# Grouped attention scores as pairs of 48-row matmuls on two row halves of the TensorE array, with the projections regrouped between the pairs

## The chip, the cores and the metric

The kernel runs on one core of one Trainium2 chip. The metric is the device time of one execution in microseconds (us), as the median of several runs. Everything below that is read per engine comes from one profiled execution.

## What is computed

A gated cross-attention block and a gated feed-forward block, on 8 batches of 256 tokens of 512 numbers, all in float32. The reference, cut to what matters:

```python
x = x + tanh(g_xattn[0]) * xattn(layernorm(x), ctx, ctx, Wq, Wk, Wv, Wfc, bfc)
x = x + tanh(g_ffn[0]) * ffn(layernorm(x), router_weight, ...)
# xattn: 32 query heads of 16, in 8 groups that share one key and one value head
score = einsum('bhqd,bhkd->bhqk', qh, kh) / sqrt(16)
out = einsum('bhqk,bhkd->bhqd', softmax(score), vh)
return out.reshape(N, S, 512) @ Wfc.T + bfc
# ffn: SwiGLU of 2048 plus a routed one of 256, weighted by the softmax of the two best logits
```

## The kernel before

**Precision.** A float32 product is made of three matmuls in the format fp32r: each operand is split into a high part (rounded) and a low part (the rest), and `three` (L1234 to L1238) adds high x low, low x high and high x high in PSUM. For the scores the same three products are one matmul: the 16 numbers of a head stand three times on the contraction rows, q as high, high, low and k as high, low, high.

**Attention.** T = 2048 tokens are 4 blocks of 512 (two batches each). A block has 8 steps: 2 batches x 4 chunks of 8 heads. Step n has 8 units. For each unit u TensorE runs:
- `sm_unit(n + 2, u)` (L1291): scores of the step two ahead with queries on the partitions, two matmuls of 256 columns into bank 0 or 1. VectorE takes their row maximum (`maximum`, L880, into `mcol`), and nothing else uses them. A maximum waits for its own unit; `sm_unit` u waits for the maximum of u - 2.
- `st_unit(n, u)` (L1301): scores of this step with keys on the partitions, one matmul of 512 columns into bank 2 or 3. A row of q_st holds minus the maximum, so the subtraction is part of the matmul (66 rows: 48 of data, filler, the row of maxima). ScalarE writes exp of them to `probs` (L733). `st_unit` u waits for the exp of u - 2.
- at u = 1 and u = 5 two `pv_unit` each (L1311): probabilities x values in four column strips of 32, bank 4. After the last of a step VectorE transposes, divides and transposes back (`o_turn` L985, `inverse` L989, `divide` L995 and L1000), ScalarE and VectorE split the result (`a_high`, `a_low`).
- at u = 2 `mt_job` (L1241): the 128 x 16 maxima of step n + 1 are turned, ScalarE copies them (`m_copy`, L652), and two DMAs put them in their row of q_st (`put_max`, L300).

**What lies between the units.** Into the units of the same body the projections of the neighbouring blocks are written by hand, a quarter of a product (`part`, three matmuls of 512 columns) at most after a unit: q of the next block (16 parts), k and v (8 parts), the output projection Wfc of this block (16 parts), and the transposes of the normalised x (`x_job`) and of v (`vt_job`). They share banks 6 and 7 (PJ). Each is followed by a high split on ScalarE and a low one on VectorE.

**DMA.** All DMAs are issued by one queue, SyncE's, in program order. q and k of a block go to DRAM (`q_scr`, `k_scr`) and come back with 16 partitions per part: `read_q` fetches the q of step n + 3 when the scores of step n - 1 are made, `read_k` the keys of a batch.

**Feed-forward.** 36 hidden blocks in pairs, with Strassen sums for gate and up, the weights split on GpSimd while the products run. GpSimd makes the split input of this stage during the last attention block, from `x2_copy` on.

## Time and profile before

| | |
|---|---|
| median of 3 runs | 955.46 us (954.95 to 959.87) |
| the profiled execution | 962.23 us, of which 960.4 us are the span of the trace |
| busy in the span: TensorE / VectorE / GpSimd / ScalarE | 916.6 / 649.1 / 485.7 / 343.8 us |
| attention: start to the first score step | 0 to 54.9 us |
| attention: blocks 0, 1, 2 | 87.6, 86.8 and 86.6 us |
| attention: block 3, to the first feed-forward product | 77.0 us |
| feed-forward | 567.5 us |

The stages are read from the table of stretches, and the boundaries are the starts of the first exp of a block. An engine's busy time is the union of its instructions. A matmul's shown length includes its way through the array, so the distance from one start to the next is what a matmul costs in a stream.

### The profile page before, as it was taken

The page shows a single profiled execution, that of the slowest core. Times are in us where ns is not written, and L with a number is a line of the kernel's source. Part 1 is how long each engine was busy: PE and PEld are TensorE (multiplying, and loading weights), DVE is VectorE, ACT ScalarE, POOL GpSimd, SP SyncE. Part 2 cuts the span into 40 slices and gives each one's busy share as a digit, 9 for nine tenths or more (in the row PEclk, how much of TensorE's full clock was granted, in tenths as well). Part 3 has the DMA queues.
Part 4 walks back from the last instruction along what each step waited for, and adds up shares of the span by engine and source line. Part 5 has one row for each costly group of instructions (what it writes and reads, how often), then busy time and mean ns, then how long its engine had stood idle before and what let it go on. Part 6 is the DMA issues. An engine that isn't in the chain of part 4 may idle for free.

```text
span 960.4 us, 14872 instructions
## 1 busy us (share of the span) xinstructions
PE 916.6 (95%) x4896; PEld 707.4 (74%) x4896; DVE 649.1 (68%) x1084; ACT 343.8 (36%) x637; POOL 485.7 (51%) x483
## 2 busy tenths in 40 slices
PE   4699999998999999989999999999999999999998
PEld 3566666676667665568888888888688888888887
DVE  6567888877877688466656665566866655666566
ACT  5156566555655577321212212134422111221111
POOL 4201301300130179785668866685588666786650
PEclk9758999999999799989999999999999999999999
DMA  7862335325353320211112121121321211212102
GB/s 272 172 165 67 85 100 89 101 68 111 77 98 77 73 44 12 87 48 61 44 44 66 44 66 44 44 67 44 110 67 45 66 44 44 65 45 64 44 1 87
DMA packets 42346, 70.83 MB, mean 74 GB/s; under 512 B 5312, under 2 KB 21184, under 8 KB 42048
## 3 DMA queue, kind: packets, MB, share of 16 engines
q1 hardware_dynamic: 42304, 70.29, 27.6%
q8 instruction: 24, 0.39, 0.2%
q14 instruction: 18, 0.15, 0.1%
HBM read 55.33 MB, written 14.68 MB: 73 GB/s over the span
## 4 chain that ended last, share of the span: by engine, by line
PE 72%; issue 17%; DVE 6%; POOL 2%; ACT 1%; DMA 1%; SPq 0%; POOLq 0%; DVEq 0%; ACTq 0%
PE bank L1236 20%; PE bank L1237 20%; PE bank L1238 20%; PE bank L1291 4%; PE bank L1311 3%; PE bank L1301 3%; PE bank L1241 2%; DVE mcol L880 1%; POOL xa L461 1%; POOL cx_l L430 1%; PE bank L1560 1%; DVE x_l L1199 1%; DMA q_st<-q_scr 1%; DMA xa<-x 1%; DVE xa L1084 0%
## 5 line engine op out<-in xcount | busy, mean ns | idle before, releaser
L880 DVE TENSOR_REDUCE mcol<-bank 128x2 f32<-128x512 f32 x256 | 170.1, 678 | 56.7 <-PE bank L1291 55.9
L1236 PE MATMUL bank<-x_l,w_h 128*128 128x512 f32 x504 | 198.1, 393 | 7.1 <-DVE u L1072 3.7
L733 ACT ACTIVATE probs<-bank 128x512 f32<-128x512 f32 x256 | 150.4, 594 | 130.2 <-PE bank L1301 129.3
L1237 PE MATMUL bank<-x_h,w_l 128*128 128x512 f32 x504 | 196.7, 390 | 0.0
L1238 PE MATMUL bank<-x_h,w_h 128*128 128x512 f32 x504 | 196.7, 390 | 0.0
L588 ACT ACTIVATE hT_h<-bank 128x512 fp32r<-128x512 f32 x72 | 43.1, 599 | 365.4 <-DVE bank L1172 356.6
L545 POOL TENSOR_TENSOR w_l<-raw,w_h 128x512 fp32r<-128x512 f32 (+1 forms) x144 | 161.9, 1157 | 2.9
L1084 DVE SCALAR_TENSOR_TENSOR xa<-bank,tgf,xa 128x512 f32<-128x512 f32 x128 | 96.2, 751 | 79.2 <-PE bank L1238 79.1
L1291 PEld LDWEIGHTS bank<-k_st,q_st 65*128 65x128 f32 x512 | 95.7, 207 | 45.6 <-DVE mcol L880 17.0
L1291 PE MATMUL bank<-k_st,q_st 65*128 65x256 f32 x512 | 117.2, 319 | 12.4 <-DMA q_st<-q_scr 8.0
L1236 PEld LDWEIGHTS bank<-x_l,w_h 128*128 128x128 f32 x504 | 94.8, 188 | 31.5 <-DVE u L1072 4.9
L430 POOL TENSOR_TENSOR cx_l<-cx_raw,cx_h 128x512 fp32r<-128x512 f32 x12 | 15.6, 1296 | 198.0 <-ACT cx_h L588 198.0
L1236 PE MATMUL bank<-dn_l,hT_h 128*128 128x512 f32 x288 | 112.8, 392 | 0.0
L1237 PE MATMUL bank<-dn_h,hT_l 128*128 128x512 f32 x288 | 112.7, 391 | 0.0
L1238 PE MATMUL bank<-dn_h,hT_h 128*128 128x512 f32 x288 | 112.6, 391 | 0.0
L1238 PEld LDWEIGHTS bank<-x_h,w_h 128*128 128x128 f32 x504 | 94.9, 188 | 19.8
L1237 PEld LDWEIGHTS bank<-x_h,w_l 128*128 128x128 f32 x504 | 94.9, 188 | 19.2
L1301 PE MATMUL bank<-q_st,k_st 66*128 66x512 f32 x256 | 105.3, 415 | 1.8 <-ACT probs L733 1.8
L1072 DVE TENSOR_TENSOR u<-bank,r 128x512 f32<-128x512 f32 x72 | 49.8, 691 | 70.9 <-PE bank L1238 70.9
L554 POOL CAST dn_h<-dnraw 128x512 fp32r<-128x512 f32 x36 | 22.0, 612 | 121.3 <-PE bank L1238 99.6
L542 POOL CAST w_h<-raw 128x1792 fp32r<-128x1792 f32 x36 | 63.6, 1767 | 28.3 <-DVE x_l L1199 16.7
L1311 PE MATMUL bank<-probs,vals 128*32 128x256 f32 x1024 | 73.7, 408 | 0.0
(146 smaller groups left out, 1376.1 us busy)
## 6 DMA issues: line engine op xcount, KB each, us to landing
raw<-w_gu SPq DMA_DIRECT2D x36, 512.0 KB, 3.3
q_st<-q_scr SPq DMA_DIRECT2D x96, 128.0 KB, 3.8
dnraw<-w_dn SPq DMA_DIRECT2D x36, 256.0 KB, 2.7
xa<-x SPq DMA_DIRECT2D x4, 1024.0 KB, 7.9
cx_raw<-ctxT SPq DMA_DIRECT2D x16, 256.0 KB, 3.5
q_scr<-qx_h SPq DMA_DIRECT2D x16, 256.0 KB, 2.1
q_scr<-qx_l SPq DMA_DIRECT2D x16, 256.0 KB, 2.2
out<-xa SPq DMA_DIRECT2D x16, 256.0 KB, 2.0
```

The source lines that it names most:

```text
L542: g.tensor_copy(w_h[f][:, :, :], raw[f][:, 0:7, :]).then_inc(gu_hi, 1)
L545: last = g.tensor_tensor(w_l[f][:, part, :], raw[f][:, part, :], w_h[f][:, part, :].bitcast(f32), ALU.subtract)
L733: nc.scalar.activation(probs[:, p, 2 * (u % 2):2 * (u % 2) + 2, :], STB[u % 2][:, :].rearrange("p (r q) -> p r q", r=2), ACT.Exp, scale=fl ...
L880: v.tensor_reduce(mcol[:, par, at:at + 2], bank[u % sm_banks(n)][:, :].rearrange("p (r k) -> p r k", r=2), AX.X, ALU.max).then_inc(max_ok, 1)
L1072: return v.tensor_tensor(out, psum[:, :], part[:, :], ALU.add)
L1084: v.scalar_tensor_tensor(tile, source[:, :], scale, tile, ALU.mult, ALU.add).then_inc(acc_ok, 1)
L1236: mm(out, a_h, b_l, start=start, stop=False, skip_group_check=onto)
L1237: mm(out, a_l, b_h, start=False, stop=False, skip_group_check=onto)
L1238: return mm(out, a_h, b_h, start=False, stop=stop, skip_group_check=onto)
L1291: last = mm(bank[u % banks][:, j * S:(j + 1) * S], q_st[0:SM, c, h, qt * P:(qt + 1) * P], k_st[0:SM, bb, 2 * c + g2, :], start=True, stop= ...
L1301: mm(STB[u % 2][:, :], k_st[0:ST, bb, 2 * c + g2, kt * P:(kt + 1) * P], q_st[0:ST, c, h:h + 2, :], start=True, stop=True).then_inc(st_full, 1)
L1311: last = mm(OTB[32 * r:32 * r + VW, g2 * S:(g2 + 1) * S], vals[:, bb, kt, 2 * c + g2, :], probs[:, p, r, :], start=kt == 0, stop=kt == 1)
```

## The change

- **Row halves.** A chunk's 8 heads are two halves of four (the columns of Wq are put in another order on the host, so that each group's heads are spread over both). Half e stands on partitions 64e to 64e + 47, its row of maxima on 64e + 48. q_st holds 4 heads side by side in place of 8, k_st the keys twice. There is no filler any more: the contraction is 48 rows for sm and 49 for st, where it was 65 and 66.
- **Pairs.** `sm_pair` v is the former units 2v and 2v + 1: four matmuls of 256 columns, alternately on the two row halves and into the two banks 0 and 1. `st_pair` is two matmuls of 512 columns. `sm_pair` v waits for the maxima of both units of pair v - 1, `st_pair` for both exps. Maxima and exps are as many and as large as before.
- **Projections.** The same parts as before, now in runs of up to four after pairs 1 and 3 only, and at other steps: after pairs 1 and 3 the parts of steps 0 to 7 of a middle block are 2+1, 1+2, 2+4, 0+4, 4+3, 3+3, 3+4 and 4+0 (q, k, v and Wfc), besides four transposes of x after each of the four places of steps 0 and 1 and two of v in steps 2 and 7. x, k and q of the later chunks use bank 6 alone, the rest bank 7.
- **ScalarE and VectorE** get the splits at other units; aT has two buffers; some splits are made one to three steps later.
- **DMA.** `read_q` is 6 DMAs of 64 KB (it was 3 of 128 KB) and waits for the probabilities x values of step n - 1; `read_k` is 6 DMAs of 128 KB (it was 3). At step 5 the queue holds 2 writes of q, 6 reads of k, 6 reads of q and 2 of maxima.
- **Start and end.** The zero fill of q_st is gone, the fill of k_st covers 128 partitions; the first weights of the feed-forward (w_h0, w_l0) have memory of their own, so GpSimd does not wait for step N - 2 before it splits them.

```diff
+CONSTS = 1
+SM = 3 * DH
 MROW = SM
 ST = MROW + 1
+ROWS = P // 2
+QUADS = HC // 2
 VW = 32
...
+        w_h0 = sb("w_h0", [P, 7, SLOT], f32r)
+        w_l0 = sb("w_l0", [P, 7, SLOT], f32r)
...
+        q_st = sb("q_st", [P, CHUNKS, QUADS, S], f32r, att)
         k_st = sb("k_st", [P, 2, GROUPS, S], f32r, att)
         vT = sb("vT", [P, BLOCK], f32, att)
...
+        aT = sb("aT", [P, 2, S], f32, att)
         tbias = sb("tbias", [P, D], f32, att)
...
-        sm_full, max_ok = sem("sm_full"), sem("max_ok")
+        sm_full, st_full, max_ok = [sem("sm_full0"), sem("sm_full1")], [sem("st_full0"), sem("st_full1")], sem("max_ok")
...
-            return bank[j] if isinstance(tb, int) and tb == 0 else PJ[j % 2]
-
-        def split_unit(s):
-
-            return 5 if s in (3, 6, 7) else 4
+            return bank[j] if isinstance(tb, int) and tb == 0 else PJ[0]
+
+        def q_bank(tb, oc):
+
+            return PJ[(oc + 1) % 2] if isinstance(tb, int) and tb == 0 else PJ[1 if oc == 0 else 0]
+
+        def f_bank(t, bb, qt):
+
+            return PJ[qt] if isinstance(t, int) and t == BLOCKS - 1 and bb == 1 else PJ[1]
...
+            def scored(n):
+
+                sp.wait_ge(pv_ok, 4 * n)
...
-                    sp.wait_ge(st_full, UNITS * n)
+                    scored(n)
                 sp.wait_ge(q_wr[c], 32 * (tb + 1))
-                for row, part in ((0, 0), (DH, 0), (2 * DH, 1)):
-                    src = q_scr[part, tb, c, :, bb * S:(bb + 1) * S].rearrange("(h d) q -> d h q", d=DH)
-                    sp.dma_start(r(q_st[row:row + DH, c, :, :]), src).then_inc(q_rd[c], 16)
+                for e in range(2):
+                    for row, part in ((0, 0), (DH, 0), (2 * DH, 1)):
+                        src = q_scr[part, tb, c, e * ROWS:(e + 1) * ROWS,
+                                    bb * S:(bb + 1) * S].rearrange("(h d) q -> d h q", d=DH)
+                        at = e * ROWS + row
+                        sp.dma_start(r(q_st[at:at + DH, c, :, :]), src).then_inc(q_rd[c], 16)
 
...
                 sp.wait_ge(k_wr, 32 * (tb + 1))
-                for row, part in ((0, 0), (DH, 1), (2 * DH, 0)):
-                    src = k_scr[part, tb, :, bb * S:(bb + 1) * S].rearrange("(g d) s -> d g s", d=DH)
-                    sp.dma_start(r(k_st[row:row + DH, bb, :, :]), src).then_inc(k_rd[bb], 16)
+                for e in range(2):
+                    for row, part in ((0, 0), (DH, 1), (2 * DH, 0)):
+                        src = k_scr[part, tb, :, bb * S:(bb + 1) * S].rearrange("(g d) s -> d g s", d=DH)
+                        at = e * ROWS + row
+                        sp.dma_start(r(k_st[at:at + DH, bb, :, :]), src).then_inc(k_rd[bb], 16)
...
-                for qt in range(2):
-                    sp.dma_start(r(q_st[MROW:MROW + 1, slot, :, qt * P:(qt + 1) * P]),
-                                 r(mT[qt * HC:(qt + 1) * HC, :])).then_inc(m_rd, 16)
+                for e in range(2):
+                    at = e * ROWS + MROW
+                    sp.dma_start(r(q_st[at:at + 1, slot, :, :].rearrange("p h (t q) -> p (h t) q", q=P)),
+                                 r(mT[e * HC:(e + 1) * HC, :])).then_inc(m_rd, 16)
 
             x_v = x.rearrange("(t j p) d -> t p j d", p=P, j=TILES)
...
                     n = STEPS * t + s
-                    if s + 3 < STEPS or not last and s != 6:
+                    if s == 0 and not first:
+                        write_q_high(t, 3)
+                        write_q_low(t, 3)
+                    if not last and s >= 5:
+                        write_q_high(t + 1, s - 5)
+                        write_q_low(t + 1, s - 5)
+                    if s == 5 and not last:
+                        read_k(t + 1, 0)
+                    if s + 3 < STEPS or not last:
                         e = s + 3
                         tb = t if e < STEPS else t + 1
                         read_q(tb, e % STEPS // CHUNKS, e % CHUNKS, n, first and s == 0)
-                    if not last:
-                        if s == 4:
-                            write_k(t + 1)
-                        if s == 6:
...
-            g.memset(q_st[0:SM, :, :, :].bitcast(f32), 0.0).then_inc(consts, 1)
...
             def split_gu(G, f):
-                if isinstance(G, int) and G < 2:
-                    pool.wait_ge(st_full, UNITS * (N - 2) if G == 0 else UNITS * N)
-                else:
+                if is_at(G, 1):
+                    pool.wait_ge(st_full[0], UNITS // 2 * N)
+                    pool.wait_ge(st_full[1], UNITS // 2 * N)
+                if not (isinstance(G, int) and G < 2):
                     pool.wait_ge(full[3], G - 1)
...
             def maximum(n, u, par):
                 qt, g2, half = u // 2 % 2, u // 4, u % 2
-                dve.wait_ge(sm_full, UNITS * n + u + 1)
+                dve.wait_ge(sm_full[half], UNITS // 2 * n + u // 2 + 1)
                 if u == 0 and not (isinstance(n, int) and n < 2):
                     dve.wait_ge(mt_tr, n - 1)
-                at = qt * HC + g2 * RH + half * 2
-                v.tensor_reduce(mcol[:, par, at:at + 2], bank[u % sm_banks(n)][:, :].rearrange("p (r k) -> p r k", r=2),
+                at = mcol[:, par, half * HC + g2 * QUADS:half * HC + (g2 + 1) * QUADS].rearrange("p (j t) -> p j t", t=2)
+                v.tensor_reduce(at[:, :, qt], bank[u % sm_banks(n)][:, :].rearrange("p (r k) -> p r k", r=2),
...
-                if not (isinstance(n, int) and n == 0):
-                    dve.wait_ge(a_lo, n)
-                v.transpose(aT[:, :], oN[:, :, :].rearrange("p b w -> p (b w)")).then_inc(at_ok, 1)
+                if not (isinstance(n, int) and n < 2):
+                    dve.wait_ge(a_lo, n - 1)
+                v.transpose(aT[:, c % 2, :], oN[:, :, :].rearrange("p b w -> p (b w)")).then_inc(at_ok, 1)
...
-            def sm_unit(n, u, bb, c):
-
-                qt, g2, half = u // 2 % 2, u // 4, u % 2
+            def sm_pair(n, v, bb, c):
+
+                qt, g2 = v % 2, v // 2
                 banks = sm_banks(n)
-                if not (isinstance(n, int) and n == 0 and u < banks):
-                    pe.wait_ge(max_ok, UNITS * n + u + 1 - banks)
+                if not (isinstance(n, int) and n == 0 and 2 * v < banks):
+                    pe.wait_ge(max_ok, UNITS * n + 2 * v + 2 - banks)
                 for j in range(2):
-                    h = g2 * RH + half * 2 + j
-                    last = mm(bank[u % banks][:, j * S:(j + 1) * S], q_st[0:SM, c, h, qt * P:(qt + 1) * P],
-                              k_st[0:SM, bb, 2 * c + g2, :], start=True, stop=True)
-                last.then_inc(sm_full, 1)
-
-            def st_unit(n, u, bb, c):
-
-                g2, kt, half = u // 4, u // 2 % 2, u % 2
-                if not (isinstance(n, int) and n == 0 and u < 2):
-                    pe.wait_ge(exp_ok, UNITS * n + u - 1)
-                h = g2 * RH + half * 2
-                mm(STB[u % 2][:, :], k_st[0:ST, bb, 2 * c + g2, kt * P:(kt + 1) * P], q_st[0:ST, c, h:h + 2, :],
-                   start=True, stop=True).then_inc(st_full, 1)
+                    for e in range(2):
+                        rows = slice(e * ROWS, e * ROWS + SM)
+                        last = mm(bank[(2 * v + e) % banks][:, j * S:(j + 1) * S],
+                                  q_st[rows, c, 2 * g2 + j, qt * P:(qt + 1) * P],
+                                  k_st[rows, bb, 2 * c + g2, :], start=True, stop=True)
+                        if j == 1:
+                            last.then_inc(sm_full[e], 1)
+
+            def st_pair(n, v, bb, c):
+
+                kt, g2 = v % 2, v // 2
+                if not (isinstance(n, int) and n == 0 and v == 0):
+                    pe.wait_ge(exp_ok, UNITS * n + 2 * v)
+                for e in range(2):
+                    rows = slice(e * ROWS, e * ROWS + ST)
+                    mm(STB[e][:, :], k_st[rows, bb, 2 * c + g2, kt * P:(kt + 1) * P],
+                       q_st[rows, c, 2 * g2:2 * g2 + 2, :], start=True, stop=True).then_inc(st_full[e], 1)
...
-                    for u in range(UNITS):
+                    for v in range(UNITS // 2):
                         if look:
-                            if u == 0:
-                                pe.wait_ge(q_rd[ce], 48 * (2 * te + be + 1))
-                                pe.wait_ge(k_rd[be], 48 * (te + 1))
-                            sm_unit(n + 2, u, be, ce)
-                        if u == 0:
+                            if v == 0:
+                                pe.wait_ge(q_rd[ce], 96 * (2 * te + be + 1))
+                                pe.wait_ge(k_rd[be], 96 * (te + 1))
+                            sm_pair(n + 2, v, be, ce)
+                        if v == 0:
                             pe.wait_ge(m_rd, 32 * (n + 1))
-                        st_unit(n, u, bb, c)
...
+                        if s == 2 and v == 3:
+                            pe.wait_ge(vt_cp, 2 * t + 2)
+                            if not first:
+                                pe.wait_ge(f_add, TILES * t)
+                            for part in (0, 1):
+                                kv_part(nx, 0, part)
+                                kv_part(nx, 1, part)
+                        if s == 3 and v == 3:
+                            for part in (2, 3):
+                                kv_part(nx, 0, part)
+                                kv_part(nx, 1, part)
+                        if s == 4 and v == 1:
+                            pe.wait_ge(v_cp, nx + 1)
+                            for part in range(DC):
+                                q_part(nx, 0, part)
+                        if s == 4 and v == 3:
```

TensorE, middle blocks, the end of step 3 and the first half of step 4, before. L1291 is a unit of scores for the maxima (sm), L1301 one for the exp (st), L1311 probabilities x values, the rows with cx_ a part of v, the row with mcol the turn of the maxima:

```order
L1291 MATMUL bank1<-k_st,q_st 128x256 x2
L1301 MATMUL bank3<-q_st,k_st 128x512
L1236 MATMUL bank7<-cx_l,wkv_h 128x512
L1237 MATMUL bank7<-cx_h,wkv_l 128x512
L1238 MATMUL bank7<-cx_h,wkv_h 128x512
L1288 ISA
L1291 MATMUL bank0<-k_st,q_st 128x256 x2
L1373 REGISTER_ALU
L1301 MATMUL bank2<-q_st,k_st 128x512
L1291 MATMUL bank1<-k_st,q_st 128x256 x2
L1301 MATMUL bank3<-q_st,k_st 128x512
L1311 MATMUL bank4<-probs,vals 32x256 x8
```

TensorE in the changed kernel, step 7 of the first block from the first pair's probabilities x values on, where L1323 is sm, L1336 st, L1346 probabilities x values and L1267 to L1269 a part of q:

```order
L1346 MATMUL bank4<-probs,vals 32x256 x8
L1323 MATMUL bank0<-k_st,q_st 128x256
L1323 MATMUL bank1<-k_st,q_st 128x256
L1323 MATMUL bank0<-k_st,q_st 128x256
L1323 MATMUL bank1<-k_st,q_st 128x256
L1336 MATMUL bank2<-q_st,k_st 128x512
L1336 MATMUL bank3<-q_st,k_st 128x512
L1272 MATMUL bank5<-ident,mcol 16x128
L1267 MATMUL bank6<-xnT_l,wq_h 128x512
L1268 MATMUL bank6<-xnT_h,wq_l 128x512
L1269 MATMUL bank6<-xnT_h,wq_h 128x512
```

Where every unit stood alone with at most one part behind it, both banks of a kind are now filled in one go, and the parts (here four in a row, of which the first is shown) follow after the turn of the maxima.

VectorE, middle blocks, step 1 from the second transpose of `divide` on, before (L880 is a maximum, L891 the sum of Wfc into x, L855 a low split):

```order
L1000 STREAM_TRANSPOSE aT<-oN 128x256
L876 REGISTER_ALU
L880 TENSOR_REDUCE mcol<-bank 128x2
L889 REGISTER_ALU
L891 ISA
L891 SCALAR_TENSOR_TENSOR xa<-bank,tgx,xa 128x512
L876 REGISTER_ALU
L880 TENSOR_REDUCE mcol<-bank 128x2
L855 TENSOR_TENSOR aT_l<-aT,aT_h 128x256
L876 REGISTER_ALU
```

and in the changed kernel the stretch behind the same transpose (L894 is a maximum, L912 the statistics of x, L905 the sum, L869 a low split):

```order
L890 REGISTER_ALU
L894 TENSOR_REDUCE mcol<-bank 128x2
L910 ISA
L912 ISA
L912 REGISTER_ALU
L912 BN_STATS stats<-xa 128x6
L894 TENSOR_REDUCE mcol<-bank 128x2
L903 REGISTER_ALU
L905 ISA
L905 SCALAR_TENSOR_TENSOR xa<-bank,tgx,xa 128x512
L875 REGISTER_ALU
L869 TENSOR_TENSOR xnT_l<-bank,xnT_h 128x4x128
```

The two maxima of a pair have the statistics between them here, and the other work comes after the pair.

## Rows read from the trace of the kernel before

**Rows 1.** The page, busy time by engine, then granted clock in 40 slices.

```profile
PE 916.6 (95%) x4896; PEld 707.4 (74%) x4896; DVE 649.1 (68%) x1084; ACT 343.8 (36%) x637; POOL 485.7 (51%) x483
...
PEclk9758999999999799989999999999999999999999
```

**Rows 2.** Table of stretches: us, busy per engine, clock, DMA share, GB/s.

```profile
0.00:54.90 54.90, 34.17 (x129) 28.15 (x129) 35.63 (x59) 17.62 (x28) 17.40 (x17) 0.81 0.73 206
54.90:142.50 87.60, 84.62 (x555) 58.95 (x553) 68.52 (x126) 50.39 (x99) 11.74 (x10) 0.88 0.45 106
142.50:229.30 86.80, 82.79 (x596) 58.59 (x596) 69.40 (x123) 50.93 (x100) 10.28 (x8) 1.00 0.41 89
229.30:315.90 86.60, 84.22 (x596) 59.30 (x596) 69.17 (x122) 50.91 (x100) 10.30 (x8) 0.98 0.42 88
315.90:392.90 77.00, 73.57 (x538) 48.03 (x537) 57.01 (x106) 49.20 (x96) 53.44 (x57) 0.93 0.24 48
```

**Rows 3.** TensorE timeline in a stream: start, length, line, tiles, count.

```profile
199.73 0.27 PE L1241 MATMUL bank<-ident,mcol 128*16 128x128 f32 x1
...
200.55 0.40 PE L1291 MATMUL bank<-k_st,q_st 65*128 65x256 f32 x2
200.79 0.40 PE L1301 MATMUL bank<-q_st,k_st 66*128 66x512 f32 x1
201.03 0.40 PE L1236 MATMUL bank<-wfc_l,aT_h 128*128 128x512 f32 x1
...
201.74 0.40 PE L1291 MATMUL bank<-k_st,q_st 65*128 65x256 f32 x2
...
203.15 0.39 PE L1301 MATMUL bank<-q_st,k_st 66*128 66x512 f32 x1
203.47 1.07 PE L1311 MATMUL bank<-probs,vals 128*32 128x256 f32 x16
204.47 0.50 PE L1236 MATMUL bank<-xnT_l,wq_h 128*128 128x512 f32 x1
204.81 0.40 PE L1237 MATMUL bank<-xnT_h,wq_l 128*128 128x512 f32 x1
```

**Rows 4.** TensorE timeline, transposes of x, then a restart after a wait.

```profile
246.23 0.60 PE L1241 MATMUL bank<-ident,xn 128*128 128x128 f32 x4
246.58 0.48 PE L1291 MATMUL bank<-k_st,q_st 65*128 65x256 f32 x2
...
251.43 0.56 PE L1291 MATMUL bank<-k_st,q_st 65*128 65x256 f32 x2 [0.47 <-DVE mcol L880]
251.79 0.63 PE L1301 MATMUL bank<-q_st,k_st 66*128 66x512 f32 x1
252.35 1.94 PE L1311 MATMUL bank<-probs,vals 128*32 128x256 f32 x16
```

**Rows 5.** VectorE timeline, one step; in brackets idle time and what ended it.

```profile
301.18 0.69 DVE L880 TENSOR_REDUCE mcol<-bank 128x2 f32<-128x512 f32 x1 [0.42 <-PE bank L1291]
...
302.60 1.25 DVE L880 TENSOR_REDUCE mcol<-bank 128x2 f32<-128x512 f32 x2
303.78 0.68 DVE L855 TENSOR_TENSOR qx_l<-bank,qx_h 128x512 fp32r<-128x512 f32 x1
304.48 0.69 DVE L880 TENSOR_REDUCE mcol<-bank 128x2 f32<-128x512 f32 x1
```

**Rows 6.** TensorE timeline, the sm unit for the first maximum of group 5.

```profile
300.74 0.40 PE L1291 MATMUL bank<-k_st,q_st 65*128 65x256 f32 x2
```

**Rows 7.** TensorE timeline, start of the program: reads of q, first scores.

```profile
39.13 4.14 PE L1291 MATMUL bank<-k_st,q_st 65*128 65x256 f32 x16 [6.24 <-DMA q_st<-q_scr]
```

**Rows 8.** DMA queue of SyncE, timeline of its issues, at the start.

```profile
29.19 1.42 SPq L295 DMA_DIRECT2D k_st<-k_scr  x3
...
31.96 4.89 SPq L283 DMA_DIRECT2D q_st<-q_scr  x6
```

**Rows 9.** DMA issues of the page: tiles, count, KB, us to landing.

```profile
q_st<-q_scr SPq DMA_DIRECT2D x96, 128.0 KB, 3.8
```

**Rows 10.** GpSimd timeline in block 3, from its first work for the feed-forward.

```profile
342.08 0.72 POOL L493 TENSOR_TENSOR xs<-xs 128x256 f32<-128x256 f32 x1 [19.90 <-ACT xs L588]
...
383.19 4.69 POOL L545 TENSOR_TENSOR w_l<-raw,w_h 128x512 fp32r<-128x512 f32 x4
387.84 0.73 POOL L528 TENSOR_TENSOR raw<-raw 128x256 f32<-128x256 f32 x1
```

**Rows 11.** TensorE timeline, block 0 at the lower clock.

```profile
64.75 0.63 PE L1291 MATMUL bank<-k_st,q_st 65*128 65x256 f32 x2
65.18 0.63 PE L1301 MATMUL bank<-q_st,k_st 66*128 66x512 f32 x1
65.61 0.63 PE L1291 MATMUL bank<-k_st,q_st 65*128 65x256 f32 x2
```

**Rows 12.** Waits of the whole span: who for whom, us, times, longest.

```profile
PEld bank L1291 <- DVE mcol L880: 17.0, 33, 2.1
```

363 lines of the change are left out of this document (190 added, 173 removed).

## The prediction

> **What bounds the kernel now.** First the busy times of the page: TensorE is busy 95% of the span, VectorE 68%, and the granted clock is nearly always at the upper level [rows 1]. Then the table of stretches. In blocks 1 and 2 TensorE is busy 82.8 and 84.2 of 86.8 and 86.6 us, VectorE 69.4 and 69.2, ScalarE 50.9 [rows 2]. So TensorE sets the pace of the attention, but VectorE is not far behind: if TensorE's work shrinks by more than 15 us a block, or if the two can overlap less, VectorE is next. The feed-forward (567.5 us) is not touched. What can move are 0 to 54.9 us (start) and the four blocks, 87.6, 86.8, 86.6 and 77.0 us [rows 2].
>
> The timeline of TensorE gives the price list [rows 3]. In a stream an sm unit of two 256-column matmuls costs 200.79 - 200.55 = 0.24 us, an st unit 0.24 us too, a part of a projection 201.74 - 201.03 = 0.71 us. A visit to the column strips (probabilities x values, two units) costs 204.81 - 203.15 less one st and one product of 0.24 us each, 1.18 us; its four rounds take (1.07 - 0.40) / 3 = 0.22 us each, 0.9 us in all, so 0.3 us go into changing the shape of the array and back.
>
> **The pairs on TensorE.** A step has 8 sm and 8 st units, 8 x 0.48 = 3.8 us. If the two halves run at once, a pair costs 0.24 + 0.24 us and the four pairs 1.9 us: 1.9 us less per step, 15.2 us per block of 8 steps. Nothing in the trace shows two row halves at work. The nearest row is the one of the column strips: there 16 matmuls take 1.07 us where each is 0.40 us long [rows 3], so strips of columns do run at once. I take full overlap for row halves; the other end is none at all, 0 us won.
> New changes of shape: an array of two row halves stands between two jobs of full height. Two of the four pairs are followed by the strips, which had their change before; the other two (maxima turn and projections behind pair 1, projections behind pair 3) each get a way in and out, 2 x 0.3 = 0.6 us per step by the row of the strips, 5 us per block. The bounds are 0 and twice that. TensorE's work per block: 84.2 - 15.2 + 5 = 74 us, 9.3 us per step.
> The weights. The four matmuls of an sm pair need four loads of 128 columns. Where loads are all that is to be done, as with the transposes of x, four of them and their short matmuls take (0.60 - 0.27) / 3 = 0.11 us each [rows 4]; 0.27 us is the length of a single one [rows 3]. If the loads for the two halves can't overlap, the sm pair takes 4 x 0.11 = 0.44 us, not 0.24, and only st wins.
> The Trainium skill says on this ("TensorE: Matmul & The Clock Gate", LDWEIGHTS) that a load takes its columns at 1.2 GHz however few rows it has, 107 ns for 128 columns, as an estimate; the 0.11 us here agree. By that rule 48 rows in place of 65 win nothing. "TensorEngine Tiling (Array Packing)", Key Properties, says that tiles can load and multiply in parallel; no row here shows it for row halves. By the first alone sm would keep its price, by both it is halved.
>
> **The wait that is new.** Before, sm unit u waited for the maximum of u - 2, so one bank was filled while VectorE read the other. Now a pair fills both banks and the next pair waits for both maxima. One round on VectorE: two maxima in a row 1.25 us from start to end [rows 5], 0.06 us to TensorE, then a cold start of the weights, 0.1 us more, and from the start of the sm unit to the maximum 301.18 - 300.74 = 0.44 us [rows 5, 6], together 1.85 us. Four rounds are 7.4 us, and with the parts of `inverse` and `divide` that do not fit into the 0.6 us gaps 7.9 us per step. That is the floor of a step, 63 us per block, where VectorE had 69 us of work spread over 87.
> On top come the runs of projections. From the start of sm pair 1 to that of sm pair 2 there are 2.1 us, of which sm, st, the maxima's turn and the changes of shape take 1.0, so 1.1 us of projection are hidden; behind pair 3 it is 1.0 us. What is longer delays the next pair. With 0.71 us per part, 0.5 us for a transposed tile of x and 0.3 us for v, the runs behind pair 1 are 1.9, 1.2, 1.7, 0, 2.8, 2.1, 2.1 and 2.8 us in steps 0 to 7, 6.8 us too long in sum; behind pair 3 they are 1.2, 1.9, 2.8, 2.8, 2.1, 2.1, 2.8 and 0.3, 8.2 us too long. VectorE's own extra work inside a pair or in excess of a gap (a low split of x before the second maximum in steps 1 and 2, statistics between maxima in steps 1, 3 and 6) is 0.6 us a piece, where no long run covers it: some 3.9 us. Sum: 63.2 + 6.8 + 8.2 + 3.9 = 82.1 us. The same kind of count gives 81 us for today's TensorE, which has 84.2 in the trace, so I add 2.5 us: **84.6 us per middle block, 2 us less than now.** Of the 10 us that TensorE is relieved of, 8 go into waiting.
> Block 0 runs its first two steps at the lower clock, where an sm and an st unit take 0.43 us each [rows 11]; halving them there wins more, some 2 us in each of the two steps. I take 84 us for 87.6. Block 3: no q, k, v to make; its first step (at the lower clock for a third of its time) gets shorter, its last two have no maxima and are paced by 8 exps. I take 73.5 us for 77.0.
>
> **The queue, the start and the end.** `read_q` now takes 6 issues. On SyncE three took 1.42 us and six 4.89 us with a wait in them [rows 8], 0.48 us each, and landing is 3.8 us after the issue [rows 9]. At step 5 sixteen issues are 7 to 8 us, and the maxima's DMAs are the last of them, so the next st pair may wait up to 1 us; I take 1 us per block, of the 2.5 us added above. At the start the keys are read as 6 DMAs before q: 3 more issues of 0.48 us and 384 KB more ahead of q on a path on which TensorE waits 6.24 us for q [rows 7]. **+2.5 us** at the start. The zero fill of q_st lies beside other work and its removal wins nothing. GpSimd's early weight split wins nothing either: it starts its chain at 342.08 when x2 comes, and has the first weights at 387.84 [rows 10], 45.8 us later, while TensorE's first product is at 392.9 [rows 2]. That leaves 5.1 us by which the last six steps of block 3 may shrink before GpSimd is the bound; the 3.5 us fit.
>
> Sum: +2.5 - 3.6 - 2.2 - 2.0 - 3.5 = -8.8 us. The profiled execution has 960.4 us of span and 962.2 in all, 6.8 us above the median of 955.5. The stages move both alike, so I take it from the median: **947 us**, 0.9% faster.
>
> **Rivals.**
> - A. *The halves do not run at once, or their weights load one after another.* If only the loads are serial, an sm pair costs 0.2 us more, and it is on the round that paces the step: 4 x 0.2 x 32 = 26 us, 973 us. If the matmuls are serial too, pairs cost as much as two units now, TensorE has 89 us a block plus waits of some 4: +6 us x 4 blocks and the start, 980 us. It decides from 0.1 us more per pair on. For it: the 0.11 us of a load. Against it: the strips overlap.
> - B. *The clock.* In the trace it fell where units and transposes stood without projections: strips at 252.35 last 1.94 us in place of 1.07 [rows 3, 4]. In the changed kernel TensorE idles more, 8 to 10 us per block. One stretch at the lower level costs about 1.5 us; with four in a block, 947 + 20 = 967 us. For it: between runs there are up to 6 us without a projection (step 3). Against: the strips are there twice a step, and 6 of 8 steps have 2 us of projections.
> - C. *The waits are smaller than my round.* The bounds are taken in series everywhere; if half of the 8 us of waiting vanish because runs and VectorE's extras fall together, and block 0 comes back to the upper clock early, a block takes 79 us: 947 - 5.6 x 4 = 925 us.
> - D. *The changes of shape eat the gain.* At twice my price they are 5 us more of TensorE a block, of which 3 lie on the path (the rest falls into waits for maxima): 947 + 12 = 959 us, 953 to 964, around no change.
>
> **How the numbers follow.** My forecast (940 to 952) 0.33, C (915 to 940) 0.25, A 0.17, B 0.10, D 0.15. What a measurement of this kernel can tell from no change is 0.5%, 4.8 us, so faster means below 950.7. Faster: 0.25 of the forecast, C, 0.02 of D and 0.01 of B, 0.53. Within: 0.08 of the forecast, 0.08 of D, 0.03 of B, 0.19. Slower: A, 0.06 of B and 0.05 of D, 0.28. Range 920 to 976: it leaves out the last of C and the serial matmuls of A.
>
> **What would show it.** The distance from an sm pair to its st pair is 0.24 to 0.26 us if loads and matmuls overlap, 0.44 or more if not. TensorE's busy time in a middle block falls to about 74 us, and waits for VectorE's maxima become its first wait, some 8 us a block (now 17.0 us in the whole span [rows 12]). VectorE's busy time stays at 69 us. First scores at about 41.5 us. GpSimd's chain in block 3 starts 8 to 10 us earlier and TensorE's first product is at 384 to 386 us. I am wrong if TensorE shows next to no waits at maxima (then C), or if blocks 1 and 2 have long stretches at the lower clock (B).

## The result and the profile after

The changed kernel takes 976.24 us (median of 4 runs, 974.12 to 976.77), the kernel before 957.66 us beside it: 1.018 times as long (95% interval 1.015 to 1.022). The forecast was 947 us with a range of 920 to 976. The sign was wrong, and the time lies just outside the range. The profiled execution of the kernel before (962.2 us) lies above its median and that of the changed kernel (974.1 us) below its own, so the tables show 11.9 of the 18.6 us between the medians.

Table of stretches of the changed kernel: start and end, length, busy time of TensorE, its weight loads, VectorE, ScalarE and GpSimd, granted clock, DMA share, GB/s. The granted clock is a mean over the stretch: 1.00 is TensorE's upper level (2.4 GHz), 0.50 the lower one (1.2 GHz). The boundaries are as in [rows 2].

```profile
0.00:55.90 55.90, 31.84 (x129) 23.98 (x129) 35.30 (x59) 17.63 (x27) 10.38 (x16) 0.82 0.66 210
55.90:146.70 90.80, 73.10 (x560) 43.48 (x564) 64.84 (x126) 48.16 (x100) 11.55 (x10) 0.89 0.47 109
146.70:236.80 90.10, 76.04 (x600) 45.61 (x596) 66.82 (x122) 48.45 (x101) 10.24 (x8) 0.94 0.41 95
236.80:325.90 89.10, 76.63 (x600) 46.38 (x593) 66.36 (x121) 48.26 (x100) 10.21 (x8) 0.92 0.42 95
325.90:406.00 80.10, 67.06 (x535) 37.34 (x534) 56.00 (x107) 47.76 (x96) 53.68 (x57) 0.89 0.25 53
406.00:972.00 566.00, 556.01 (x2490) 453.43 (x2486) 349.22 (x553) 124.80 (x215) 382.77 (x384) 1.00 0.17 55
```

Against [rows 2] TensorE has 7 to 8 us less to do in each of blocks 1 and 2, as was meant, and yet the blocks are 3.3 and 2.5 us longer; the start costs 1.0, block 0 3.2 and block 3 3.1 us. What was saved is idle now, and more. The granted clock of the blocks is 0.89 to 0.94 where blocks 1 and 2 had 1.00 and 0.98.

Block 2 cut into its eight steps shows where:

```profile
236.78:245.62 8.84, 8.30 (x82) 5.00 (x78) 7.97 (x16) 7.74 (x15) 0.00 (x0) 1.00 0.33 101
245.62:261.31 15.69, 10.04 (x78) 5.67 (x70) 8.76 (x17) 7.07 (x15) 2.54 (x2) 0.78 0.67 95
261.31:271.75 10.44, 9.57 (x81) 5.96 (x85) 8.76 (x17) 5.36 (x13) 0.00 (x0) 1.00 0.28 89
271.75:284.46 12.71, 11.09 (x73) 6.58 (x76) 8.60 (x16) 5.83 (x13) 7.67 (x6) 0.73 0.12 32
284.45:294.76 10.31, 10.03 (x82) 6.29 (x86) 8.12 (x16) 6.10 (x13) 0.00 (x0) 1.00 0.34 115
294.76:305.33 10.57, 9.40 (x79) 5.71 (x83) 7.22 (x14) 4.96 (x10) 0.00 (x0) 1.00 1.01 187
305.34:316.27 10.93, 10.07 (x82) 6.31 (x86) 8.48 (x16) 5.39 (x12) 0.00 (x0) 1.00 0.26 85
316.27:325.93 9.66, 8.18 (x75) 4.87 (x78) 8.51 (x18) 5.85 (x13) 0.00 (x0) 1.00 0.23 69
```

Two of eight steps stick out: step 1 with 15.7 us and step 3 with 12.7 us, both with the clock down. (Step 1 of block 1 takes 16.4 us, but its step 3 takes 10.4 us at a clock of 1.00.) The other six sum to 60.8 us, 10.1 us each.

Step 1. The timelines of TensorE, ScalarE and SyncE around 250 us (start, length, what, idle time before it and who ended it):

```profile
254.47 0.79 PE L1336 MATMUL bank<-q_st,k_st 49*128 49x512 f32 x2 [4.91 <-ACT probs L739]
255.19 1.93 PE L1346 MATMUL bank<-probs,vals 128*32 128x256 f32 x16
```

```profile
245.62 1.09 ACT L739 ACTIVATE probs<-bank 128x512 f32<-128x512 f32 x2
252.81 0.63 ACT L594 ACTIVATE cx_h<-cx_raw 128x512 fp32r<-128x512 f32 x1 [6.10 <-DMA cx_raw<-ctxT]
253.35 1.07 ACT L739 ACTIVATE probs<-bank 128x512 f32<-128x512 f32 x2
```

```profile
243.49 2.72 SPq L311 DMA_DIRECT2D k_st<-k_scr  x6
246.49 0.92 SPq L278 DMA_DIRECT2D cx_raw<-ctxT  x2
```

After the second exp of the step ScalarE stands 6.1 us in front of `cx_h`, the high split of the next block's context. The exps are queued behind it, the next st pair waits 4.9 us for an exp, and what TensorE does next runs at the lower level (the probabilities x values in their column strips take 1.93 us, as at 252.35 in [rows 4]). The context was asked for at 246.49, behind six reads of keys.

In the kernel before there was room. SyncE's queue there, one block start earlier (229.3), and ScalarE's split:

```profile
235.14 1.30 SPq L295 DMA_DIRECT2D k_st<-k_scr  x3
236.72 0.89 SPq L267 DMA_DIRECT2D cx_raw<-ctxT  x2
```

```profile
244.68 0.61 ACT L588 ACTIVATE cx_h<-cx_raw 128x512 fp32r<-128x512 f32 x1
```

Counted from the start of the block: before, the loads are issued after 7.4 us, are there 4.1 us later (11.5) and are wanted after 15.4. After the change they are issued after 9.7 us, are there 6.2 us later (15.9), and are wanted after 9.9 (246.7 - 236.8), since step 0 takes 8.8 us in place of 11.2 and `cx_h` follows the second exp, not the third. The load came 4.4 us later and the need 5.5 us earlier. The view of the tile cx_raw has the times from issue to landing, first before, then after:

```profile
DMA to landing us min/median/max: 4.1/4.4/4.8
```

```profile
DMA to landing us min/median/max: 6.2/6.4/6.7
```

The waits of the whole span (total, times, longest), which answer to [rows 12]:

```profile
PEld bank L1323 <- DVE mcol L894: 63.4, 73, 3.0
...
PE bank L1323 <- DVE mcol L894: 30.9, 44, 2.7
...
ACT cx_h L594 <- DMA cx_raw<-ctxT: 16.5, 3, 6.3
PE bank L1336 <- ACT probs L739: 15.7, 8, 5.2
PE bank L1323 <- DMA q_st<-q_scr: 13.0, 6, 6.6
```

The wait for maxima came as was said. Its size depends on the row: TensorE's weight loads, the row of [rows 12], wait 63.4 us, some 16 us a block and twice the 8 that were said; the matmuls themselves wait 30.9 us, 7.7 us a block. 6.6 us of the last line are the start (6.24 in [rows 7]); of the rest, 6.4 us, 5.2 are q at the start of step 6 of blocks 0 to 2 (2.4, 1.9 and 0.9), behind the six key reads of step 5, and 1.0 is at step 2 of block 3. In the kernel before there was one such wait, of 1.7 us.

### The profile page after: what moved, and what is told of

It reads as the page before. It is cut to its first block, busy times and chain, and to the rows that moved or that the text cites. A ratio compares the mean times of both kernels' runs of the same rounds, so it can differ in the third digit from the quotient of the medians.

```text
span 972.3 us, 14886 instructions
## 1 busy us (share of the span) xinstructions
PE 880.7 (91%) x4896; PEld 650.2 (67%) x4896; DVE 638.5 (66%) x1084; ACT 335.1 (34%) x637; POOL 478.8 (49%) x482
## 4 chain that ended last, share of the span: by engine, by line
PE 70%; DVE 12%; DMA 7%; SPq 5%; issue 4%; ACT 2%; POOL 0%; DVEq 0%; ACTq 0%; POOLq 0%
PE bank L1267 21%; PE bank L1268 20%; PE bank L1269 20%; DVE mcol L894 5%; PE bank L1323 4%; DMA q_st<-q_scr 2%; SPq L297 2%; SPq L311 2%; PE bank L1346 2%; PE bank L1336 2%; PE bank L1272 2%; DMA q_scr<-qx_l 2%; DMA cx_raw<-ctxT 1%; PE bank L1622 1%; ACT probs L739 1%
## 5 line engine op out<-in xcount | busy, mean ns | idle before, releaser
L894 DVE TENSOR_REDUCE mcol<-bank 128x2 f32<-128x512 f32 x256 | 166.9, 676 | 77.6 <-PE bank L1323 77.3
L1267 PE MATMUL bank<-x_l,w_h 128*128 128x512 f32 x504 | 198.0, 393 | 7.1 <-DVE u L1103 3.6
L1269 PE MATMUL bank<-x_h,w_h 128*128 128x512 f32 x504 | 196.7, 390 | 0.0
L739 ACT ACTIVATE probs<-bank 128x512 f32<-128x512 f32 x256 | 138.9, 595 | 132.7 <-PE bank L1336 132.4
L1267 PEld LDWEIGHTS bank<-x_l,w_h 128*128 128x128 f32 x504 | 94.7, 188 | 31.5 <-DVE u L1103 4.8
L1323 PE MATMUL bank<-k_st,q_st 48*128 48x256 f32 x512 | 70.4, 358 | 47.0 <-DVE mcol L894 30.9
L1267 PE MATMUL bank<-dn_l,hT_h 128*128 128x512 f32 x288 | 112.3, 390 | 0.0
L1269 PE MATMUL bank<-dn_h,hT_h 128*128 128x512 f32 x288 | 112.2, 389 | 0.0
L1323 PEld LDWEIGHTS bank<-k_st,q_st 48*128 48x128 f32 x512 | 42.8, 207 | 100.2 <-DVE mcol L894 63.4
L1269 PEld LDWEIGHTS bank<-x_h,w_h 128*128 128x128 f32 x504 | 94.9, 188 | 19.8
L1346 PE MATMUL bank<-probs,vals 128*32 128x256 f32 x1024 | 76.1, 419 | 0.0
L1336 PE MATMUL bank<-q_st,k_st 49*128 49x512 f32 x256 | 56.7, 438 | 16.2 <-ACT probs L739 15.7
```

The source lines that it names most:

```text
L739: nc.scalar.activation(probs[:, p, 2 * half:2 * half + 2, :], STB[half][:, :].rearrange("p (r q) -> p r q", r=2), ACT.Exp, scale=float(DH) ...
L894: v.tensor_reduce(at[:, :, qt], bank[u % sm_banks(n)][:, :].rearrange("p (r k) -> p r k", r=2), AX.X, ALU.max).then_inc(max_ok, 1)
L1267: mm(out, a_h, b_l, start=start, stop=False, skip_group_check=onto)
L1269: return mm(out, a_h, b_h, start=False, stop=stop, skip_group_check=onto)
L1323: last = mm(bank[(2 * v + e) % banks][:, j * S:(j + 1) * S], q_st[rows, c, 2 * g2 + j, qt * P:(qt + 1) * P], k_st[rows, bb, 2 * c + g2, :] ...
L1336: mm(STB[e][:, :], k_st[rows, bb, 2 * c + g2, kt * P:(kt + 1) * P], q_st[rows, c, 2 * g2:2 * g2 + 2, :], start=True, stop=True).then_inc(s ...
```

## Experiments

All times are medians beside runs of the kernel before on the same chip; the ratio is to it, with its 95% interval. The rows do not all come from the same chip; beside them the kernel before had medians of 955.7 to 957.7 us and a mean clock of 0.975. Differences of 2 us between rows mean nothing.

| kernel | us | ratio | mean granted clock |
|---|---|---|---|
| changed kernel | 976.2 | 1.018 (1.015 to 1.022) | 0.953 |
| same_half | 1016.5 | 1.060 (1.052 to 1.067) | 0.933 |
| cx_first | 967.3 | 1.012 (1.005 to 1.018) | 0.962 |
| keys_step4 | 980.7 | 1.023 (1.016 to 1.031) | 0.956 |
| cx_keys | 974.1 | 1.019 (1.013 to 1.025) | 0.954 |
| cx_early | 969.7 | 1.010 (1.006 to 1.015) | 0.964 |
| cx_fill | 961.2 | 1.005 (1.001 to 1.008) | 0.968 |
| even_only | 967.3 | 1.011 (1.007 to 1.015) | 0.964 |
| cx_even | 955.2 | 0.997 (0.993 to 1.000) | 0.970 |
| last_spread | 957.3 | 1.000 (0.996 to 1.003) | 0.969 |
| x_late | 957.0 | 1.000 (0.997 to 1.004) | 0.969 |
| x_late_fill | 951.6 | 0.995 (0.992 to 0.999) | 0.978 |
| cx_even_fill | 957.3 | 1.003 (1.000 to 1.006) | 0.971 |
| before_dma | 959.2 | 1.002 (0.999 to 1.006) | 0.972 |
| before_fill | 951.3 | 0.997 (0.995 to 1.000) | 0.983 |

Two theories stand against each other. **Q**: the queue. Doubled key reads delay what stands behind them, and an engine stands with its in-order queue. **B**: the clock. The regrouping leaves stretches in which TensorE has little to do, and the granted clock falls there. A third, that the halves do not run at once, is tried first.

**Do the halves overlap?** same_half puts both halves on the first row half:

```diff
-                        rows = slice(e * ROWS, e * ROWS + SM)
+                        rows = slice(0, SM)
...
-                    rows = slice(e * ROWS, e * ROWS + ST)
+                    rows = slice(0, ST)
```

> The changed kernel with all score matmuls on the first row half (rows 0 to 47 and 0 to 48 for both halves): the same number of matmuls, rows and columns, but nothing to run beside. The scores of the second four heads are left out (the first four are computed twice). It measures what the side-by-side running is worth. If the two halves overlap as the trace reads (0.24 us from sm pair to st pair), each sm pair and each st pair costs 0.24 us more: 32 x 4 x 0.48 = 61 us of TensorE. The sm part lies on the round sm - maxima - sm, the st part is partly hidden in the waits for maxima (8 us a block), so 1005 to 1037 us. If the halves brought nothing, the time stays at 976 us.

1016.5 us, 40 us more than the changed kernel. The pairs on TensorE's timeline, first in the changed kernel, then in same_half, both at the upper clock level and after other work:

```profile
199.51 0.50 PE L1323 MATMUL bank<-k_st,q_st 48*128 48x256 f32 x4
199.85 0.40 PE L1336 MATMUL bank<-q_st,k_st 49*128 49x512 f32 x2
200.19 0.50 PE L1267 MATMUL bank<-xnT_l,wq_h 128*128 128x512 f32 x1
```

```profile
211.37 0.74 PE L1323 MATMUL bank<-k_st,q_st 48*128 48x256 f32 x4
211.95 0.63 PE L1336 MATMUL bank<-q_st,k_st 49*128 49x512 f32 x2
212.50 1.07 PE L1346 MATMUL bank<-probs,vals 128*32 128x256 f32 x16
```

From sm pair to st pair 0.34 against 0.58 us, from st pair to the next 0.34 against 0.55. These are no chosen places: at the upper level, where nothing is waited for, the first distance is 0.34 us in all 39 places of the changed kernel and 0.55 to 0.58 in all 61 of same_half. That is 0.24 and 0.21 us saved per pair, with the two halves' weight loads inside: both halves load and multiply at once. The mechanism of the change works, and rival A is out. The time lies in the expected 1005 to 1037 us, though the 0.24 us that the expectation names as the distance in the trace are 0.34; since same_half also has the lower clock (0.933), the 40 us are not all the pairs' own. ("TensorEngine Tiling (Array Packing)", Key Properties, in the Trainium skill says that tiles can load and multiply in parallel; these rows agree with it.)

**The queue alone.** cx_first swaps two things in step 0:

```diff
+                    if s in (0, 2) and not last:
+                        load_cx(t + 1, s)
+                        load_cx(t + 1, s + 1)
                     if s == 0:
                         if not first:
                             scored(n)
                         read_k(t, 1)
-                    if s in (0, 2) and not last:
-                        load_cx(t + 1, s)
-                        load_cx(t + 1, s + 1)
```

> The changed kernel with one move on SyncE's queue: in step 0 the two loads of the next block's context (load_cx) stand ahead of the six reads of keys (read_k) instead of behind them. The bytes and the number of DMAs are the same. Theory Q (the queue): in step 1 ScalarE stands 6.1 us in front of cx_h, whose input lies behind 768 KB of keys; the exps behind it and then TensorE stand with it, step 1 takes 12.6, 16.4 and 15.7 us in blocks 0, 1 and 2. With the loads first step 1 should take about 10.5 us in blocks 1 and 2 and 11 to 12 in block 0, ScalarE's wait for cx_raw should be under 1 us, and the time should fall by 2 x 5.5 + 1 to 2 = 12 to 14 us, to 962 to 965 us. Rival W (the pairs): the long step 1 is the wait for both maxima and the lower clock, and ScalarE's wait is only where it shows; then the time moves by less than 3 us, 973 to 977 us.

967.3 us: 9 us won, under the 12 to 14 expected. ScalarE's wait for cx_raw is gone from the list of waits. Steps 1 and 3 of block 1 and of block 2:

```profile
157.64:169.81 12.17, 8.25 (x78) 4.87 (x81) 8.45 (x17) 7.28 (x15) 2.57 (x2) 1.00 0.88 134
181.84:192.22 10.38, 8.04 (x73) 4.76 (x76) 7.77 (x16) 5.82 (x13) 7.62 (x6) 1.00 0.14 40
246.04:257.65 11.61, 9.46 (x78) 5.72 (x70) 8.59 (x17) 7.17 (x16) 2.56 (x2) 0.85 0.82 125
268.13:281.51 13.38, 11.03 (x73) 6.72 (x76) 8.60 (x16) 5.82 (x13) 7.68 (x6) 0.74 0.10 30
```

Step 1 of blocks 1 and 2 falls from 16.4 and 15.7 us to 12.2 and 11.6, as Q says, by 4 us each, though not to the 10.5 expected. Step 1 of block 0 does not fall to 11 to 12 but rises from 12.6 to 13.9 us. There the reads of q, which stand behind the keys and the 1 MB load of x, are the next to be late: q is there 22 to 23 us after the start of the block in both kernels, and TensorE, which now comes earlier, waits 5.9 us for it at the start of step 2 (0.5 in the changed kernel). In block 1 this wait is 2.2 us. The one of block 0:

```profile
78.35 0.80 PE L1323 MATMUL bank<-k_st,q_st 48*128 48x256 f32 x4 [5.88 <-DMA q_st<-q_scr]
```

So the stall of ScalarE had hidden a second one, and part of the gain is given back to it.

In the table above, the second and the fourth row are the same step of the same program in one execution, with the same 73 matmuls: 10.4 us at a clock of 1.00, 13.4 us at 0.74. So the lower clock goes with 3.0 us more there, all of it in TensorE's busy time (8.0 and 11.0 us), and whether it falls is not the same in each block.

Three attempts on the rest of the queue. keys_step4 and cx_keys issue the next block's first keys behind `write_k` of step 4; cx_early lets the reads wait for the st pairs of step n - 1 instead of for its probabilities x values.

```diff
-                    if s == 5 and not last:
-                        read_k(t + 1, 0)
...
                         write_k(t + 1)
+                        read_k(t + 1, 0)
```

> The changed kernel with the six reads of the next block's first keys (read_k(t + 1, 0)) issued at the end of step 4, behind the writes of k, instead of in step 5 ahead of the reads of q. Theory Q: the waits for q at the start of step 6 (1.9 us in block 1, 0.9 us in block 2) go, and the part of the clock's fall behind them: 2 to 5 us in all, 971 to 974 us. Rival: the queue now waits for k to be written and its landing (2 to 3 us) with the writes of q and the reads of q behind it, so that step 5's q comes late instead; then no change or 1 to 3 us slower, 976 to 979 us.

> Both moves together: context loads ahead of the key reads in step 0, and the first keys of the next block read at the end of step 4. Theory Q: the two waits are at different places, so the gains add: 12 to 14 and 2 to 5 us, 957 to 962 us, that is the time of the kernel before. If theory W holds (waits for maxima and clock), 971 to 976 us.

> cx_first with the old condition for reading q and the keys: read_q and read_k(t, 1) wait for the st pairs of step n - 1 instead of for its probabilities x values, which TensorE runs only after the first pair of the next step. Each read_q can start some 1.5 to 2 us earlier. Theory Q: the reads are the last thing that step 6 waits for (0.6 to 3.0 us for q_st), and everything behind them on the queue moves up: 2 to 4 us faster than cx_first, 963 to 965 us. Rival: at step 5 read_q is held by the writes of q and by the six key reads, not by that wait, so 966 to 968 us.

keys_step4 takes 980.7 us, 4 us more than the changed kernel, and cx_keys 974.1, 7 us more than cx_first: in both, theory Q's times are missed and the move costs what its stated rival says or a bit more. Steps 5 of blocks 1 and 2 take 14.5 and 13.5 us in keys_step4 (11.7 and 10.6 in the changed kernel). The queue in block 1 of keys_step4:

```profile
207.72 3.99 SPq L311 DMA_DIRECT2D k_st<-k_scr  x6
211.80 0.38 SPq L282 DMA_DIRECT2D q_scr<-qx_h  x1
212.36 0.37 SPq L286 DMA_DIRECT2D q_scr<-qx_l  x1
217.47 3.09 SPq L297 DMA_DIRECT2D q_st<-q_scr  x6
```

The writes of q now stand behind the key reads, and the reads of q wait 5 us for those writes to land. In the changed kernel the key reads lie in just that wait. cx_early's 969.7 us are no different from cx_first's 967.3, and Q's 963 to 965 are missed. In block 1 of its trace the second write of q is issued at 204.56, the six key reads from 205.08 and the reads of q from 208.05 on, without a wait between them: the writes and the keys hold the reads, as its rival had it.

**Is the traffic enough by itself?** before_dma gives the kernel before the same reads (the second copy goes to rows that nothing reads).

```diff
+                    sp.dma_start(r(k_st[ST + row:ST + row + DH, bb, :, :]), src).then_inc(k_rd[bb], 16)
```

> The kernel before with the changed kernel's traffic: read_k is six DMAs of 128 KB (the second copy goes to rows 66 to 113 of k_st, which nothing reads), read_q six of 64 KB (the same bytes as before in twice as many DMAs). Nothing else moves. It measures the disputed cost by itself. Theory Q: the doubled keys delay the context loads behind them by 3 x 1.1 us and by as many issues, ScalarE's cx_h at the third exp of step 1 waits, and q of the next block comes later at step 6: 2 to 5 us per block in blocks 0 to 2, so 6 to 12 us slower than before, 963 to 968 us beside 956.7. Rival: the traffic is covered in the old order, since there k is read in step 4, the projections need x and q ahead of ctx, and it only hurts together with the new order: 956 to 959 us.

1.002, with 1 in the interval: the doubled reads cost at most 0.6% there, and no cost is shown. With the old order nobody wants the context before 15.4 us into the block. So it is not the traffic alone but the traffic together with the earlier need: a shorter step 0 and an earlier place in ScalarE's order. (No run changes the need alone.)

**The clock.** Step 3 has no projection behind pair 1 and four behind pair 3; step 2 has four behind pair 3. cx_even (on top of cx_first) moves two of them; even_only does it without cx_first. cx_fill leaves them and puts four useless matmuls in the empty place.

```diff
                         if s == 2 and v == 3:
...
-                            for part in (0, 1):
-                                kv_part(nx, 0, part)
-                                kv_part(nx, 1, part)
+                            kv_part(nx, 0, 0)
+                            kv_part(nx, 1, 0)
+                        if s == 3 and v == 1:
+                            kv_part(nx, 0, 1)
+                            kv_part(nx, 1, 1)
```

```diff
+                            if s == 3 and not last:
+                                for part in range(4):
+                                    mm(TPB[:, P:], wq_h[:, 0, 0:P], wq_h[:, 1, 0:3 * P], start=True, stop=True,
+                                       skip_group_check=True)
                             mt_job(n + 1, (s + 1) % 2)
```

> cx_first with four useless matmuls of 384 columns (0.16 us each, 0.64 us in all) into an unused part of bank 5 ahead of the turn of the maxima in step 3 of blocks 0 to 2, where no projection stands. Theory B: if it is the thin stretch of TensorE that lets the clock fall, step 3 stays at 10.4 to 11.0 us in all three blocks, where cx_first has 13.4, 10.4 and 13.4: up to 6 us gained for 1 to 2 us of added work, 962 to 965 us. Rival: the fall has another cause (the load before it), step 3 still falls to the lower clock at the same places: 967 to 970 us.

> cx_first with one pair of parts moved: of the four parts of k and v behind pair 3 of step 2, two go behind pair 1 of step 3, where nothing but the turn of the maxima stands. The parts of steps 2 and 3 are then 2+2 and 2+4 in place of 2+4 and 0+4. Theory B (the clock falls where scores stand for some 6 us without a projection): step 3 no longer has the stretch at the lower clock that it has in one to two of three blocks, and is 10.4 us or a bit more in all blocks in place of 13.4; step 2 gets 1.0 to 1.4 us shorter; step 3, with 1.4 us more of parts, some 0.5 to 1 us longer at the upper clock. In sum 3 to 6 us faster than cx_first (967.3): 961 to 964 us. Rival W (VectorE's round is the floor and runs only fill it): step 2 shorter, step 3 longer by the same, 966 to 968 us, with the clock as before.

> The changed kernel with only the move of two parts of k and v from behind pair 3 of step 2 to behind pair 1 of step 3; the queue is left as in the changed kernel. cx_first alone won 9 us and both moves 21 us. If the clock and the queue are two causes that add, this one wins 10 to 12 us by itself: 964 to 967 us, with step 1 of blocks 1 and 2 still at 15 to 16 us. Rival: the low clock of step 3 was only a late effect of the stall in step 1, and without the queue's repair the move wins 1 to 4 us, 972 to 975 us.

cx_fill takes 961.2 us: 6 us faster than cx_first by doing 1.9 us more work (962 to 965 were expected). (The two ran on different chips, and the intervals of their ratios overlap. cx_early, which is as fast as cx_first and ran beside cx_fill, took 969.7.) Step 3 of block 0 in cx_first, then of blocks 0, 1 and 2 in cx_fill:

```profile
90.61:104.01 13.40, 11.06 (x73) 6.74 (x77) 8.37 (x17) 5.82 (x13) 2.55 (x2) 0.75 0.12 31
```

```profile
90.92:101.33 10.41, 8.86 (x77) 5.39 (x81) 8.36 (x17) 5.87 (x13) 2.56 (x2) 1.00 0.15 40
176.94:187.33 10.39, 8.84 (x77) 5.40 (x80) 7.83 (x16) 5.96 (x13) 7.51 (x6) 1.00 0.15 40
263.44:273.87 10.43, 8.88 (x77) 5.40 (x80) 7.83 (x16) 5.95 (x13) 7.54 (x6) 1.00 0.13 39
```

In block 1, where cx_first had held the clock too, there are 0.8 us more of busy time and the same length; in blocks 0 and 2 step 3 is 3.0 us shorter each, 6.0 of the 7.2 us between the two profiled spans.

One profile of each could be chance, since the clock does not fall in every block. All profiles together say more. In the five kernels that have nothing behind pair 1 of step 3 (the changed one, cx_first, keys_step4, cx_keys, cx_early), the clock fell in 8 of the 15 steps 3 of blocks 0 to 2, which took 12.6 to 13.4 us at 0.73 to 0.75; the other 7 took 10.4 us at 1.00. In the seven kernels with parts or useless matmuls there, all 21 took 10.4 to 10.6 us at 1.00. That the thin stretch lets the clock fall is shown by this, at this place.

cx_even takes 955.2 us, 12 us less than cx_first, twice the upper end of what was expected. even_only takes 967.3, 9 us less than the changed kernel (10 to 12 were expected), so the gains add within the noise (9 + 9, together 21), and the rival that step 3 only suffers from step 1 is out: in even_only step 1 is still at 15.9 and 15.6 us. Steps 1 to 3 of block 2 in cx_even:

```profile
237.42:248.10 10.68, 7.97 (x78) 4.71 (x70) 8.58 (x17) 7.17 (x16) 2.55 (x2) 1.00 0.89 132
248.10:257.40 9.30, 8.27 (x75) 4.83 (x78) 8.73 (x17) 5.34 (x12) 0.00 (x0) 1.00 0.32 100
257.40:267.98 10.58, 9.35 (x79) 5.74 (x83) 8.18 (x16) 5.90 (x12) 7.27 (x6) 1.00 0.14 38
```

Step 2 loses 1.1 us and step 3 gains 0.2 at the upper clock: the overlong run behind pair 3 of step 2 is gone, and step 3's wait for maxima takes the parts in for nothing. This is the second effect of the move, beside the clock. The eight steps of this block sum to 80.6 us (86.6 before) with TensorE busy 71.6.

**Block 3 and block 0.** last_spread (on top of cx_even) gives step 3 of block 3 two parts of Wfc, one behind pair 1 and one behind pair 3; x_late (on top) issues the 1 MB load of x a step later in block 0; x_late_fill (on top) puts the useless matmuls into steps 0 to 2 of block 0, where blocks 1 and 2 have Wfc and block 0 has nothing; cx_even_fill has that fill without the two moves, and before_fill has it in the kernel before.

```diff
-                            if s == 4 and v == 1:
+                            if s == 3 and v == 1:
+                                pe.wait_ge(vt_cp, 2 * t + 2)
                                 pe.wait_ge(f_add, TILES * t)
                                 f_part(t, 0, 0, 0)
+                            if s == 3 and v == 3:
                                 f_part(t, 0, 0, 1)
-                            if s == 4 and v == 3:
+                            if s == 4 and v == 1:
                                 f_part(t, 0, 0, 2)
```

```diff
-                    if s == 0 and first:
+                    if s == 1 and first:
                         sp.dma_start(xa[:, T // P - TILES:T // P, :], x_v[BLOCKS - 1]).then_inc(in_x[BLOCKS - 1], 16)
```

> cx_even, and in block 3 the four parts of Wfc for its first 128 tokens stand in steps 3, 3, 4 and 5 instead of 4, 4, 4 and 5 (step 3 had none). Theory B: block 3 has 7.8 us at the lower clock in step 3 and 2.5 us in step 4 of cx_even; with a projection in each place these go: step 3 falls from 11.9 to 10 us or less, step 4 from 10.9 to 9.5 us, 2 to 4 us in all, 951 to 953 us. Rival: what is long there is the wait for ScalarE's copy of the maxima and VectorE's 9.6 us of work in step 3 beside GpSimd's 11.6 us; then 954 to 956 us.

> last_spread, and in block 0 the 1 MB load of the last block's x is issued at the end of step 1 instead of at the end of step 0. There it stood ahead of the q reads of step 1 (issued 66.1 to 68.8 us, landed 74.8 to 76.7), and TensorE waited 3.4 us for q at the start of step 2, with the lower clock after it (12 us of it in step 2). Theory Q: the wait goes, step 2 of block 0 falls from 12.2 to under 11 us and step 1 from 12.7 to about 11: 2 to 5 us faster than last_spread. Rival: block 0 is at the lower clock because it has no Wfc parts, whatever the queue does; then under 1 us.

> x_late, and in steps 0 to 2 of block 0, where the other blocks have Wfc parts, four useless matmuls of 384 columns (0.64 us) behind pair 1, and behind pair 3 of steps 0 and 1. Theory B: block 0 stays at the upper clock from its start, steps 0 to 2 last 9.5, 10.5 and 9.5 us instead of 10.5, 12.7 and 12.2: 3 to 5 us faster than x_late. Rival: the useless work costs its 3.2 us on the path and the clock falls as before: 1 to 3 us slower than x_late.

> cx_even with the useless matmuls in block 0 and without the moves of last_spread and x_late. If the fill is the only part of x_late_fill that brings something, it has the same time, 950 to 953 us. If the fill works only when the q wait at step 2 of block 0 is gone (x_late), this kernel stays at 954 to 957 us.

> The kernel before with the same useless matmuls as x_late_fill (four of 384 columns ahead of the turn of the maxima in steps 0 to 2 of block 0, four more behind unit 6 of steps 0 and 1). Before has 20.5 us at the lower clock in block 0 and steps 0 and 1 of 11.8 and 12.8 us. If the fill holds the clock there as well, 2 to 4 us faster than before, 953 to 955 us, and the pairs' own share of the gain is what is left between this kernel and x_late_fill. If the old order, with a unit at a time, keeps the clock at the lower level regardless, 1 to 3 us slower, 958 to 960 us.

last_spread (957.3) and x_late (957.0) bring nothing against cx_even's 955.2; the times that theory B expected for block 3 and Q for block 0 are both missed. In x_late's profile steps 1 and 2 of block 0 did fall as Q had it, to 9.8 and 9.1 us (12.5 and 10.4 in last_spread), but the median did not follow. x_late_fill takes 951.6 us and is faster than both kernels of this case, by 0.5% (0.1 to 0.8) against before; it is the best of the twelve variants of the changed kernel, so some of that may be luck. cx_even_fill, 957.3, is not faster, and before_fill gets 951.3 us (0.3%, 0.0 to 0.5) from the same useless matmuls in the old kernel. Steps 0 to 2 of block 0 there:

```profile
52.62:63.24 10.62, 9.03 (x56) 6.97 (x55) 7.46 (x15) 7.21 (x14) 0.00 (x0) 0.84 0.66 132
63.24:72.92 9.68, 9.22 (x75) 6.83 (x76) 7.99 (x15) 8.28 (x18) 2.81 (x2) 1.00 0.83 203
72.92:82.86 9.94, 9.94 (x76) 7.40 (x75) 8.62 (x17) 5.85 (x12) 0.00 (x0) 1.00 0.38 93
```

30.2 us where the kernel before has 34.0, and the clock falls in the first of the three alone. So about as much as x_late_fill wins could be had without the change. In x_late_fill itself the profile does not show where the gain lies: its filled steps take 12.65, 10.45 and 9.11 us (x_late: 10.94, 9.83 and 9.10), and what is shorter is block 3, whose steps 3 and 4, the same in both programs, take 10.3 and 9.3 us at a clock of 1.00 (x_late: 12.3 and 10.6). Why the fill helps with x_late and not without it stays open.

**What the clock is worth over all runs.** Of the runs of the kernel before beside these, 81 lie between 947 and 963 us, with mean clocks of 0.966 to 0.984: 19 runs at 0.970 or less have a mean of 960.3 us, 18 runs at 0.980 or more 951.5. A line through the 81 gives 6.3 us per 0.01 of mean clock (correlation -0.87). By that line the kernel before would take 970.0 us at the changed kernel's mean clock of 0.953, so 14 of the 19.8 us between the means go with the clock, and 5.8 are left. With the nine longer runs (up to 967 us) in it the line is steeper, 7.1 us per 0.01, and 3.7 us are left; and either way 0.953 lies below every clock that the line was drawn through. By the first line cx_even at 0.970 is 3.2 us below, x_late_fill 2.2 below, before_fill 0.7 above. It is a correlation: a stall lowers the clock and costs time itself. As an estimate it puts what the change is worth with both defects mended at 2 to 3 us, not 9.

A second estimate comes from the two tables of stretches. By their clocks TensorE spends 63 us of the four blocks at the lower level in the changed kernel and 35 in the kernel before. In step 3 of cx_first's block 2 some 7 us at the lower level went with 3.0 us more. At that rate the 28 us more are worth 12 us, as much as the two profiled spans differ by; it is an upper bound, since time that TensorE spends waiting costs no more at the lower level.

## Why the prediction was wrong

- **The pairs on TensorE: right.** Full overlap of matmuls and loads. The price of a change of shape was too high: an sm and an st pair before a stream of parts take 0.34 + 0.34 us (199.51 to 200.19), 0.48 of it their own work, so the way in and out costs 0.2 us per place instead of the 0.3 taken. The distance from sm pair to st pair, 0.34 us, lies between the two signs that were named (0.24 to 0.26 with overlap, 0.44 or more without), because half of this price is in it; only same_half's 0.58 decides it. Busy time was to fall to 74 us; it is 76 in the changed kernel with its slow stretches, and 71.6 in cx_even's block 2 at the upper clock.
- **The wait that is new: right in kind, somewhat too large.** Waits for maxima are TensorE's first wait. A middle block was put at 84.6 us (the runs behind pair 3, as listed there, add up to 8.7 us too long, not 8.2, which would make it 85.1); where nothing is late, the clock holds and the parts are spread (cx_even, block 2) it takes 80.6 us, near rival C's 79.
- **The start: too large.** +2.5 us were taken, +1.0 measured; first scores at 39.79 us, not 41.5. One profile hardly measures this term: in the experiments that leave the start as it is in the changed kernel they come at 37.9 to 41.9 us.
- **The queue: the step that failed.** "I take 1 us per block" priced only step 5, where the waits for q behind it came to 5.2 us in blocks 0 to 2. Step 0 was not looked at: its key reads doubled as well, the context loads stand right behind them on SyncE's queue, and ScalarE's `cx_h` moved from behind the third exp to behind the second. That cost some 4 us in step 1 of each of blocks 1 and 2 (cx_first), part of it by the clock after the stall. The timeline of before showed the slack, 3.9 us between landing (11.5) and need (15.4), and what the change took from it (2.3 us later issue, 2.1 us slower landing, a step 0 that is 2.4 us shorter, `cx_h` an exp earlier) came to 9.9 us. The prediction made step 0 faster and did not ask what was then late.
- **Rival B was the other half, and had 0.10.** It was priced at 20 us for four stretches in a block; the clock's share is some 12 to 14 us by the estimates above. The price of one stretch, 1.5 us, was half of what step 3 shows (3.0 us), and the number of them too high. The row named for it, "up to 6 us without a projection (step 3)", is the place where it fell. The mistake was to let the strips and the projections of the other steps speak against a fall in that one.
- **Block 3** was to take 73.5 us and took 80.1: its steps 3 and 4, of which step 3 has no projection, ran at 12.4 and 12.3 us instead of 8.8 and 8.9. Their clock was 0.60 and 0.71:

```profile
355.57:367.98 12.41, 10.06 (x69) 5.40 (x73) 9.47 (x16) 7.17 (x15) 12.04 (x13) 0.60 0.12 34
367.97:380.29 12.32, 11.11 (x78) 6.45 (x82) 7.64 (x14) 7.17 (x14) 9.25 (x11) 0.71 0.12 33
```

  last_spread did not mend it (step 3 takes 12.3 us at 0.62 there), so the missing parts are not shown to be its cause. In x_late_fill, with the same block 3 as x_late, it did not happen. It stays open.
- **GpSimd** was not the bound: its first weights are split at 398.0 us, TensorE's first product is at 406.0, right behind its last attention work, and the feed-forward takes 566 us (567.5 before). GpSimd's chain starts at 348.1 us, 6 us later than before and not 8 to 10 us earlier. VectorE's busy time, said to stay at 69 us, is 67 and 66 in blocks 1 and 2.

In sum: -8.8 us expected, +18.6 measured. The steps that failed are the queue's term, which left out the context loads of step 0, and the clock, which the sum put at nothing; the two defects give 21 us (cx_even against the changed kernel), which leads from 976.2 to 955.2. The 8 us from there to 947 are not explained by any single run here; what is long in cx_even against the prediction is steps 5 and 6 with their late q, block 3, and block 0 with its low clock. That the forecast's own terms would have come true without the two defects is not shown.

## What to carry to other kernels

When a change makes a stage shorter, list what that stage had covered: for each transfer in the queue, its landing and its first use, counted from the stage's start, before and after. When a change moves small work out of a thin stretch of TensorE into a run elsewhere, the relief may be paid for in clock. Spread the parts evenly first, and count a saved microsecond of TensorE only when the row of that step still shows a clock of 1.00. A comparison of two kernels is easier to read with the mean clock of each run beside its time.

## What was not expected of the hardware

- Row halves of 48 rows overlap, weight loads included: 0.34 us for four loads and four matmuls of 256 columns between other work, 0.58 us when both halves use the same rows.
- The same step of one program in one execution takes 10.38 us at a granted clock of 1.00 and 13.38 us at 0.74; over 81 runs of one kernel 0.01 of mean clock goes with 6.3 us of 956.
- 1.9 us of useless matmuls, 0.64 us in each of three steps, made a kernel 6 us faster (967.3 and 961.2 us).
